# Last stage of a transformer kernel: values projected once per tile and brought back through device memory; queries and keys squared and rotated straight from two alternating PSUM banks

## The reference, cut to what matters

```python
def local_attention(q, k, v):            # window 32: each query sees its window and the one before
    bk2, bv2 = look(bk), look(bv)        # 64 keys and values per window of 32 queries
    sim = jnp.einsum('bhwie,bhwje->bhwij', bq, bk2) * QK_SCALE
    attn = jax.nn.softmax(jnp.where(mask, -big, sim), -1)
    return jnp.einsum('bhwij,bhwje->bhwie', attn, bv2)

def attn_layer(x, Wqkv, qs, ksc, Wo):
    q, k, v = jnp.split(x @ Wqkv, 3, -1)             # 16 heads of 64
    q, k = l2norm(q) * qs, l2norm(k) * ksc
    q = q * cos * scale + rotate_half(q) * sin * scale
    k = k * cos / scale + rotate_half(k) * sin / scale
    return local_attention(q, k, v) @ Wo

for i in range(6):
    x = attn_layer(shift_tokens(x), ...) + x
    x = ffn_layer(shift_tokens(x), ...) + x
```

## Time and profile before

| | us |
|---|---|
| median of 3 runs | 2362.76 |
| the three runs | 2357.71, 2362.76, 2363.86 |
| the profiled execution | 2356.89 |
| its span | 2355.1 |
| PE busy | 1965.8 (83%) |
| DVE busy | 1724.7 (73%) |
| ACT busy | 1438.1 (61%) |
| POOL busy | 906.3 (38%) |

### The profile page before, as it was taken

The page is one execution under the profiler, slowest core; times in us unless marked ns, Lnnn a source line. Parts: engine busy times, 40 slices in busy tenths (PEclk is TensorE's granted clock), DMA queues, the critical chain, the costliest instruction groups (busy, mean ns, idle before and its releaser), DMA issues. The chain is left out here.

```text
span 2355.1 us, 52980 instructions
## 1 busy us (share of the span) xinstructions
PE 1965.8 (83%) x19088; PEld 921.9 (39%) x19088; DVE 1724.7 (73%) x3041; ACT 1438.1 (61%) x2138; POOL 906.3 (38%) x913
## 2 busy tenths in 40 slices
PE   5745888888888888888848998988988989898896
PEld 3531222222222222222224554654654555565564
DVE  4744677777777767777559978878878878887783
ACT  4311566666665656666627766767757758666673
POOL 0011111111111111111039757747647657666670
PEclk9855899999998989999959999999999999999998
DMA  1013222222323232222010000000000000000000
GB/s 33 1 30 63 42 60 54 57 53 54 59 54 59 54 59 54 59 54 56 2 61 2 2 31 11 13 32 11 13 32 11 12 32 11 12 31 12 12 3 10
DMA packets 52107, 77.07 MB, mean 33 GB/s; under 512 B 10900, under 2 KB 45750, under 8 KB 48054
## 3 DMA queue, kind: packets, MB, share of 16 engines
q1 hardware_dynamic: 49781, 73.27, 13.7%
q10 hardware_dynamic: 2112, 0.94, 0.2%
HBM read 47.70 MB, written 25.69 MB: 31 GB/s over the span
## 5 line engine op out<-in xcount | busy, mean ns | idle before, releaser
L899 DVE TENSOR_REDUCE ENM<-PM 128x1 f32<-128x512 f32 x1024 | 658.7, 686 | 258.4 <-PE PM L722 249.3
L819 ACT ACTIVATE EPT<-PA 128x1024 f32<-128x1024 f32 x512 | 512.4, 1021 | 223.3 <-PE PA L734 140.0
L722 PE MATMUL PM<-EKX,EQX 48*128 48x512 bf16 x1024 | 356.0, 402 | 104.9 <-DVE ENM L899 84.3
L1215 POOL TENSOR_TENSOR DQR<-DR 128x512 f32<-128x512 f32 x192 | 245.8, 1280 | 316.1 <-DVE DR L1507 302.8
L1217 POOL TENSOR_TENSOR DRN<-DRN,DHALF 128x8 f32<-128x8 f32 x192 | 346.2, 1803 | 11.0
L642 POOL CAST ENMP<-ENM 128x16 bf16<-128x16 f32 x64 | 12.6, 196 | 789.2 <-DVE ENM L899 789.2
L744 PE MATMUL PV<-EPT,EVP 128*32 128x512 f32 x2048 | 286.3, 632 | 0.9 <-ACT EPT L819 0.7
L734 PE MATMUL PA<-EQX,EKX 51*128 51x512 bf16 x1024 | 254.4, 396 | 29.1 <-DMA EQX<-EROWS 16.3
L722 PEld LDWEIGHTS PM<-EKX,EQX 48*128 48x128 bf16 x1024 | 85.5, 94 | 483.3 <-DVE ENM L899 392.1
L1261 PE MATMUL PM<-DWQKV,DXS 128*128 128x512 f32 x384 | 213.9, 640 | 36.5 <-ACT XNT L1464 21.9
L1438 ACT ACTIVATE DV<-PM 64x512 f32<-64x512 f32 x384 | 225.5, 587 | 6.8 <-PE PM L1274 4.5
(11 more groups left out here) (208 smaller groups left out, 3061.4 us busy)
## 6 DMA issues: line engine op xcount, KB each, us to landing
e_park<-EPARTS SPq DMA_DIRECT2D x64, 192.0 KB, 2.9
EQX<-e_park SPq DMA_DIRECT2D x32, 384.0 KB, 5.6
EKX<-e_park SPq DMA_DIRECT2D x32, 384.0 KB, 9.1
DWQKV<-in_WqkvR SPq DMA_DIRECT2D x6, 1536.0 KB, 6.3
e_park<-EPARTS SPq DMA_DIRECT2D x64, 128.0 KB, 2.7
e_park<-EPARTS SPq DMA_DIRECT2D x64, 64.0 KB, 2.1
EQX<-EROWS ACTq DMA_DIRECT2D x256, 3.0 KB
DWO<-in_WoR SPq DMA_DIRECT2D x6, 512.0 KB, 3.6
```

The source lines that it names most:

```text
L722: pe.matmul(PM[:, r, :], lhsT=QX[64 * r:64 * r + KQ, b, hp, t * 128:(t + 1) * 128], rhs=KX[64 * r:64 * r + KQ, b, hp, :], start=True, stop ...
L819: s_.activation(PT[:, kt, pair * 2 * S:(pair + 1) * 2 * S], PA[:, 2 * pair:2 * pair + 2, :].rearrange("p a b -> p (a b)"), ACT.Exp, scale= ...
L899: v.tensor_reduce(NM[:, g % 2, t, j, 0:1], PM[:, r, :], AX.X, ALU.max, negate=True).then_inc(maxed, 1)
L1215: g.tensor_tensor(qr, r1, r2, ALU.add).then_inc(roped.sem if queries else joined.sem, 1)
```

## The change

Three things change together.

1. Values: the tile's values are projected once, 128 tokens x 512 columns, in parts c = 0 (even heads) and c = 2 (odd heads) only. ACT copies them to a new tile `VT`; SP stores `VT` to device memory (`vpark`) at the end of the step, and reads it back in the next step into `V`, laid out by window with each token twice. `V` now has three buffers, and `mix` waits for `vloaded` in place of a drained bank.
2. Banks: queries are projected into bank 0 and keys into bank 1; the values of part 0 go to bank 1 and those of part 2 to bank 0.
3. `RAW` is gone. ACT squares the bank directly, and DVE rotates directly from the bank, after waiting for ACT's square. The bank is free for PE when DVE has rotated (`free_pm`).

```diff
+        if 1 <= k <= NT:
+            order.append((k, 5, "vin", k - 1))
...
+        if k < NT:
+            order.append((k, 48, "vout", k))
...
-        RAW, SQ = m.sb("DRAW", [128, 2, 512]), m.sb("DSQ", [128, 2, 512])
+        SQ = m.sb("DSQ", [128, 2, 512])
...
+                def vout(layer, n):
...
+                    sp.dma_start(vpark[b, W + t * 128:W + (t + 1) * 128, :, :].rearrange("p r e -> p (r e)"),
+                                 VT[:, n % 2, :, :].rearrange("p r e -> p (r e)")).then_inc(vparked, 16)
+                def vin(layer, n):
...
+                    for par in range(2):
+                        for half in range(2):
+                            at = t * 128 + W * half
+                            dst = V[64 * par + W * half:64 * par + W * half + W, n % 3, :, par, :, :].rearrange("p w h e -> p w (h e)")
+                            src = vpark[b, at:at + 4 * W, par, :].rearrange("(w j) e -> j w e", j=W)
+                            sp.dma_start(dst, src).then_inc(vloaded, 16)
...
+                    def free_pm(i, use_):
+                        before = pm[i].previous(layer, use_)
...
+                        if kind == "qk":
+                            pe.wait_ge(rotated.sem, rotated.at(at, k))
+                        else:
+                            pe.wait_ge(pm_out[i].drained, pm_out[i].number(at, (kind, k)))
+                        pe.sem_inc(pe_passed, 1)
...
-                            free(pm0, ("qk", k))
-                            pe.matmul(PM[:, 0, :], lhsT=XS[:, b, W + t * 128:W + (t + 1) * 128], rhs=WQKV[:, c * 512:(c + 1) * 512],
+                            i = c // 2
+                            free_pm(i, ("qk", k))
+                            pe.matmul(PM[:, i, :], lhsT=XS[:, b, W + t * 128:W + (t + 1) * 128], rhs=WQKV[:, c * 512:(c + 1) * 512],
...
-                        if n < NT:
-                            free(pm1, ("v", k))
-                            keys = XS[:, b, k % 16 * W:(k % 16 + 2) * W]
-                            for par in range(2):
-                                mm = pe.matmul(PM[64 * par:64 * par + 64, 1, :], lhsT=keys, rhs=wv[:, par], start=True, stop=True)
+                        if n < NT and c % 2 == 0:
+                            i = 1 - c // 2
+                            free_pm(i, ("v", 2 * n + c // 2))
+                            pe.matmul(PM[:, i, :], lhsT=XS[:, b, W + t * 128:W + (t + 1) * 128], rhs=wv[:, c // 2],
...
-                            s.activation(RAW[:, k % 2, :], PM[:, 0, :], ACT.Copy).then_inc(pm0.drained, 1)
+                            i = c // 2
+                            wait(summed, k - 2)
+                            s.activation(SQ[:, k % 2, :], PM[:, i, :], ACT.Square).then_inc(squared.sem, 1)
...
-                            for par in range(2):
-                                r = slice(64 * par, 64 * par + 64)
-                                ins = s.activation(V[r, n % 4, c, :, par, :], PM[r, 1, :].rearrange("p (h e) -> p h e", h=HP), ACT.Copy)
+                        if n < NT and c % 2 == 0:
+                            s.activation(VT[:, n % 2, c // 2, :], PM[:, i, :], ACT.Copy).then_inc(pm_out[i].drained, 1)
...
-                        x = RAW[:, k % 2, :].rearrange("p (h e) -> p h e", h=8)
+                        i = c // 2
+                        x = PM[:, i, :].rearrange("p (h e) -> p h e", h=8)
...
-                        dve.wait_ge(pm0.drained, pm0.number(layer, ("qk", k)))
+                        stands(pm[i], ("qk", k))
+                        wait(squared, k)
```

More of the change, by code:

```diff
@@ L1039, in layer_order @@
         s, o = k - 2, k - 3
+        if k == PERIOD:
+            order.append((k, -5, "early", None))
         if 0 <= s < NT:
             order.append((k, 0, "score", s))
+        if 1 <= k <= NT:
+            order.append((k, 5, "vin", k - 1))
         if k in (0, TB):
@@ L1089, in number, with previous @@
         return before + (self.body.index((back, use_)) + 1)
+    def previous(self, layer, use_):
+        back = int((1, use_) in self.body)
+        body = layer + back
+        order = self.body
+        if isinstance(body, int):
+            order = self.first if body == 0 else self.last if body == DEPTH else self.body
+        i = order.index((back, use_))
+        if i:
+            return body - order[i - 1][0], order[i - 1][1]
+        if isinstance(body, int) and body == 0:
+            return None
+        return body - 1 - self.body[-1][0], self.body[-1][1]
 def stage_d(nc, shared, d, V, out):
@@ new lines, in piece @@
+                def piece(layer, name, n, nxt):
+                    if name == "vout":
+                        vout(layer, n)
+                    elif name == "vin":
+                        vin(layer, n)
+                    elif name == "early" and nxt is not None:
+                        sp.wait_ge(pm[1].filled, pm[1].number(layer, ("qk", 4 * NT - 1)))
+                        sp.sem_inc(sp_passed, 1)
+                        sp.wait_ge(tables.sem, tables.at(layer, 0))
+                        sp.sem_inc(sp_passed, 1)
+                        early(nxt)
+                    elif name == "output" and nxt is not None:
+                        sp.wait_ge(pv.filled, pv.number(layer, ("out", NT - 1)))
+                        sp.sem_inc(sp_passed, 1)
+                        output(nxt)
+                    elif name == "late" and nxt is not None:
+                        sp.wait_ge(y_done.sem, y_done.at(layer, B - 1))
+                        sp.sem_inc(sp_passed, 1)
+                        late(nxt)
@@ L1175, in _ @@
                 late(slice(0, 1))
+                sp.wait_ge(padded, 3)
+                for b in range(B):
+                    sp.dma_start(vpark[b, 0:W, :, :].rearrange("j r (q e) -> (j r q) e", e=HP * W),
+                                 KT[:, b, :, 0:W]).then_inc(zeroed, 16)
+                sp.wait_ge(zeroed, 32)
+                for back, name, n in FIRST:
+                    piece(0, name, n, None)
                 with sp.Fori(1, DEPTH) as layer:
                     nxt = bass.ds(layer, 1)
[L1179 to L1185, removed]
+                    for back, name, n in BODY:
+                        piece(layer - back, name, n, nxt)
+                for back, name, n in LAST:
+                    piece(DEPTH - back, name, n, None)
                 sp.wait_ge(finished, NT)
```

91 lines of the change are left out of this document (60 added, 31 removed).

## The result

The changed kernel takes 2434.62 us (median of 4 runs, 2434.34 to 2438.77), the kernel before on the same chip 2361.61 us: a ratio of 1.0315, 95% interval 1.0297 to 1.0333. It is slower, by 73 us and not by 8; 2371 us was forecast, with 2387 as the upper end.

A forecast was written before the change was run, and what follows sets the result against it. PE is busy all 17.4 us of a full step, with DVE close behind at 15.8, so the waits between them matter. Terms 15 + 5 - 6 - 6 = +8 us on 2356.9 gave 2365, 2371 on the median's scale; range 2344 to 2387.

The forecast's parts named there:

- full steps (5 and 6): Alike steps mid-layer in the last stage, 13 counted: PE's new wait and likely clock drop cost +15 us.
- step 7: Six times, feed-forward norm between DVE's second and third rotation: fourth projection 4.7 us late, partly absorbed; +5 us in all.
- step 4: Six times, first projection of a batch's second half waits for the shifted tile: 1.0 us stays won, -6 us (0 to -9).
- steps 0 to 3, first tiles: Where DVE and POOL lead and most held-up rotations lie: a fifth of 30.5 us won, -6 us (+3 to -14).
- store and loads: One store and four loads per tile through SP: landing in time for the mix, with a step to spare; cost 0.
- PE is freed of 97 us: Value projections in the last stage: 2.0 us less PE work a step, over 48 tiles; the gain if PE alone set the pace.
- ACT costs nothing: ACT loses the RAW copy and three of four pairs of V copies; it does not set the end, costed at nothing.
- The 30.5 us of held-up rotations go: DVE's rotations in the last stage: those from SBUF are sometimes held up, from PSUM not; 30.5 us expected to go.
- The new wait and the clock in a full step: Second projection waits 2.0 us for DVE's rotation: step 17.9 us, or 18.8 if the clock falls (8 in 10).
- the clock holds in full steps: Rival, 2 in 10: no clock drop in full steps, only 13 x 0.46; sum -1, or 2362 us.
- the held-up time is on the path: Rival, 3 in 10: faster, half of 30.5 us won back in steps 0 to 3 and first tiles; -19, 2344 us.
- The loads are late: Rival, under 1 in 20, within the slower case: the mix waits 1 us in each of 48 steps, 2411 us.

The follow-up runs named there:

- e3: The changed kernel without the store of VT, the loads into V and the waits on them (mix reads zeros): 2408.2 us, ratio 1.0197 to before.
- e1: The kernel before with only the values part: projected once per tile through device memory, RAW and fixed banks kept; 2329.7 us, ratio 0.9862.
- e9: The changed kernel with ACT's copy to RAW back, alternating banks kept, without the values' store and loads (mix reads zeros): 2348.9 us, ratio 0.9976.
- e2: The kernel before with only the alternating banks and rotations straight from PSUM, no RAW, values projected per window as before: 2452.2 us, ratio 1.0383.
- e4: The kernel before with values projected once per tile, RAW kept, without the store and loads (mix reads zeros): 2320.6 us, ratio 0.9835.
- e10: The changed kernel with SP issuing the loads of the values only after the mix of the same step: 2410.2 us, ratio 1.0229.

## Why the prediction was wrong

The sign was right and the wait is the one that was foreseen; the size was off: +8 forecast, +77.7 in the spans. Its own sum, term by term, with what the trace of after has for it (sums of steps over all layers, less those of before) and how much of that is time in which PE paused (all of `issue`, less that of before); then the same for e3, without the traffic:

| term | forecast | after | of it pauses | e3 | of it pauses |
|---|---|---|---|---|---|
| full steps (5 and 6) | +15 | +40 | +34 | +20 | +10 |
| step 7 | +5 | +23 | +13 | +20 | +10 |
| step 4 | -6 | -10 | -5 | -10 | -5 |
| steps 0 to 3, first tiles | -6 | +19 | +5 | +28 | +11 |
| step 8 and the end | none | +17 | +8 | +4 | +2 |
| store and loads | 0 | in the others | | | |
| ahead of the stage | none | -11 | | -10 | |
| sum | +8 | +78 | +56 | +51 | +28 |

The terms are rounded one by one. Within the stage the loss is 88 us, 80 more than forecast.

- **PE is freed of 97 us**: right. In e1 PE is busy for 906 us of the last stage and not for 1006. It is worth 1.4%, not the 4% that it would be if PE alone set the pace.
- **ACT costs nothing**: right for the work. But its copy was what let PE go on, and that was the half of the change that cost.
- **The 30.5 us of held-up rotations go**: right (longest 693 and 417 ns, where the earlier trace rows have 1690 and 1506). But they did not reach the end of the stage, since L1614 took 42 us. The prediction had counted this for full steps ("so I take 2.66 for the three parts left") and not for the others, where it nevertheless credited 6 us. By the Trainium skill's rule (SBUF — State Buffer, "Who interferes with whom") the trace agrees on the rotations; the 2332 us that it would have given did not come.
- **The new wait and the clock in a full step**: right, as far as it went. Place, length of the wait and start of the projection came out within 0.1 us in e3. Step 5 of e3, which has no pause, takes 19.4 us where the granted clock fell and 18.1 and 18.3 us where it did not (18.8 and 17.9 forecast). That the sum of both full steps came near, +20 against +15, is partly luck: 10 of the 20 are pauses, and the clock fell in 6 of the 13 full steps and not in 8 of 10. In the changed kernel itself the wait at the second projection is shorter (1.00 us), because PE now comes late to it from a pause.
- **"Cost 0" for the store and the loads, and no term for PE's pauses**: the first failed step, and the largest. The store and the loads were weighed as something the mix waits for, and the mix does not wait for them, as forecast. They cost 26 us in another way, by PE's pauses, which are 27 us shorter without them (77 and 50). The other 27 us of pauses above those of before (50 and 23) are there without any traffic; only the kernels with both parts of the change have them (e3 50 and e9 46, against e2 24 and e4 29). Where they come from stays open. Together the pauses make 56 of the 80 us, if each costs its own length, as the pairs of kernels above nearly show.
- **"Steps 0 to 3 ... a fifth of it, -6"** (+3 to -14): the second failed step. They lost 19 us, 5 of them pauses. The term was made from DVE's gain, which L1614 took back, without PE's waits. Step 2 has the longest waits for a rotation (46 of the 142 us, up to 6.0 each), and its granted clock is 0.75 to 0.82 in layers 1 to 5, where it was 1.00; yet it lost only 6 us. Step 3 lost 11, of which e1, without the new banks, has 3; what the other 8 are no run isolates.
- **Step 8** did not stand in the sum at all: it lost 16 us, 8 of them pauses; without the traffic it lost 4.
- **Step 7, "part is absorbed, since DVE is late there in any case"** (+5, bounds 0 and +12): the wait was put at 4.7 us late and is 4.56, and most of it is absorbed, as forecast. The excess is the pause in the score behind it: 13 of the 23 us. In e10, which has 2 us of pauses there, the step lost 9, and in layer 0, without a pause, 0.6. The wait does not make the pause: e2 has 28 us of such waits in step 7 and no pause, e1 has no such wait and 6 us of pauses there.
- **The rivals**: that the clock holds in full steps is out: in the changed kernel it fell in 10 of 13, and the mean of the stage is 0.92 against 0.97. That the held-up time is on the path is out by the table. "The loads are late" had a part of the cause and the wrong victim; its price of 1 us a step, 2411, was the nearest of all the figures given. What would show the prediction wrong, steps 0 to 3 shortened or full steps under 17.4 us, did not happen: the ways in which it could be too low were not listed.

## What to carry to other kernels

Before a copy out of PSUM is dropped, ask which engine's queue will then free the bank, what the longest other piece in that queue is (here the norm, 4.1 us from its first instruction to its last), and what PE did ahead of time while it ran; if the bank must be held that long, let the next user be two parts behind and not one. A late engine did absorb most of the longest wait here, but not the pause that fell behind it. And the price of a transfer is not only its own landing: add up the idle time of PE that has no releaser before and after a change, and try to keep bulk loads away from those places (here 31 us of the stage).

## What the runs showed of the hardware that I had not expected

- PE's pauses without a releaser sit at the same matmuls in layers 1 to 4, which are passes of one loop body. In steps 5 and 6, while the loads of the values run, they are 1.9 to 3.4 us, and with the loads moved (e10) 0.8 to 1.5 us. A packet of 16 KB of the queue named "instruction" lies at 29 of the 34. The longest, 4.3 to 4.9 us in step 8, come at a DMA share of 0.02 to 0.03.
- The time at a lower clock and the total time do not go together. e1 has a mean granted clock of 0.94 in the window of the last stage (before: 0.97), and is the faster of the two:

```profile
1225.00:2432.00 1207.00, 905.65 (x12816) 606.29 (x12816) 892.78 (x1576) 602.05 (x1032) 723.35 (x516) 0.94 0.29 79
```
